# The check of the weights' low halves, two pieces at a time as 32-bit integers

## What is computed

```python
FP4_GRID = jnp.array([0.0, 0.5, 1.0, 1.5, 2.0, 3.0, 4.0, 6.0])
idx = jnp.argmin(jnp.abs(jnp.abs(v)[..., None] - FP4_GRID), axis=-1)
codes = jnp.sign(v) * FP4_GRID[idx]
...
w = codes * jnp.repeat(scales, block_size, axis=0)   # x @ w for q, k, v and the output
```

## Time and profile before

| | |
|---|---|
| runs | 1265.62, 1264.48, 1261.58 us |
| span of the profiled execution | 1275.3 us (no other time of that execution is given) |
| PE busy | 1182.9 us, 93% |
| VectorE, ScalarE, POOL busy | 911.6, 865.0, 664.7 us |
| chain that ended last | PE 64%, DMA 11%, VectorE 10%, issue 7%, ScalarE 6% |
| mean granted TensorE clock | 0.982 |

### The profile page before, as it was taken

How to read it: one execution, slowest core, us unless ns; L and a number is a source line. 1 busy time by engine, 2 the same in 40 slices (tenths; PEclk the granted TensorE clock), 3 DMA queues, 4 the chain that set the end, 5 groups by cost and what they waited for, 6 DMA issues and landing times.

```text
span 1275.3 us, 25192 instructions
## 1 busy us (share of the span) xinstructions
PE 1182.9 (93%) x7600; PEld 836.2 (66%) x7600; DVE 911.6 (71%) x2651; ACT 865.0 (68%) x2316; POOL 664.7 (52%) x746
## 2 busy tenths in 40 slices
PE   3899999999999999999999999999879798989985
PEld 1466666766666676676667666677535477868863
DVE  4887688799789889979988987887757232223336
ACT  3999779878878887887887788788625232323413
POOL 4564334336654655654664565466562523444557
PEclk9999999999999999999999999999989899999998
DMA  7686577867976665565566457456428379898676
GB/s 270 160 213 143 113 131 151 168 151 170 197 174 140 118 123 102 105 123 104 101 108 109 88 97 141 73 100 106 83 58 249 112 207 247 219 234 217 144 197 215
DMA packets 394759, 190.01 MB, mean 149 GB/s; under 512 B 317521, under 2 KB 373303, under 8 KB 394625
## 3 DMA queue, kind: packets, MB, share of 16 engines
q1 hardware_dynamic: 375040, 173.53, 59.7%
q0 software_dynamic: 16416, 11.70, 5.1%
q10 hardware_dynamic: 3168, 3.15, 0.7%
HBM read 75.32 MB, written 64.69 MB: 110 GB/s over the span
## 4 chain that ended last, share of the span: by engine, by line
PE 64%; DMA 11%; DVE 10%; issue 7%; ACT 6%; another core or an unknown queue 1%; SPq 1%; POOL 1%; ACTq 0%; DVEq 0%; POOLq 0%
PE bank L1144 15%; PE bank L1173 14%; PE bank L1188 11%; DMA Y<-W,wix 9%; PE bank L1159 7%; PE bank L1205 7%; PE bank L1237 3%; PE bank L1312 2%; PE bank L1325 2%; PE bank L1355 1%; DVE nm L1581 1%; PE bank L1271 1%; ACT P L1414 1%; DVE PH L1574 1%; DMA X<-in_x 1%
## 5 line engine op out<-in xcount | busy, mean ns | idle before, releaser
L1414 ACT ACTIVATE P<-bank,nm 128x256 f32<-128x256 f32 x512 | 237.9, 471 | 107.3 <-DVE nm L1581 97.1
L1144 PE MATMUL bank<-RB,W 128*128 128x512 f16 x1076 | 275.1, 381 | 5.3 <-DVE W L812 3.9
L1173 PE MATMUL bank<-RB 128*128 128x256 f32 x1024 | 244.6, 382 | 10.2 <-issue 6.9
L1074 POOL TENSOR_SCALAR P<-P,rr 128x256 f32<-128x256 f32 x256 | 121.1, 482 | 252.5 <-DVE rr L1563 244.2
L823 POOL DMA_INDIRECT BUF<-RT,ix x192 | 201.6, 1050 | 72.8 <-issue 37.6
L1173 PEld LDWEIGHTS bank<-RB 128*128 128x128 f32 x1024 | 185.7, 191 | 34.9 <-ACT RB L1385 6.6
L1144 PEld LDWEIGHTS bank<-RB,W 128*128 128x128 f16 x1076 | 105.2, 98 | 123.4 <-issue 8.8
L1581 DVE TENSOR_REDUCE nm<-bank 128x2 f32<-128x512 f32 x256 | 174.2, 681 | 11.0 <-PE bank L1173 8.8
L1205 PE MATMUL bank<-W,O 128*128 128x256 f16 x1060 | 158.8, 275 | 5.2 <-DVE O L1587 5.2
L1095 POOL DMA_INDIRECT Y<-W,wix x64 | 90.9, 1421 | 117.8 <-ACT W L1492 67.5
L1079 POOL TENSOR_TENSOR PH<-P,PH 128x512 f16<-128x512 f32 x86 | 101.2, 1176 | 87.3 <-ACT PH L1430 86.3
(11 more groups left out here) (224 smaller groups left out, 1995.4 us busy)
## 6 DMA issues: line engine op xcount, KB each, us to landing
RB<-in_ewT SPq DMA_DIRECT2D x24, 352.0 KB
BUF<-zrow SPq DMA_DIRECT2D x24, 321.0 KB, 3.3
W<-BUF SPq DMA_DIRECT2D x64, 120.4 KB
HT<-in_ewT SPq DMA_DIRECT2D x18, 352.0 KB
HT<-in_wc SPq DMA_DIRECT2D x24, 256.0 KB, 4.2
HT<-in_ws SPq DMA_DIRECT2D x24, 256.0 KB, 4.7
Y<-zrow SPq DMA_DIRECT2D x20, 256.0 KB
RB<-in_ewd SPq DMA_DIRECT2D x24, 176.0 KB
```

What stands on the lines that cost most here:

```text
L1074: r = eng.tensor_scalar(p, p, rr[:, w % 4, t:t + 1], SP_, ALU.mult, ALU.mult)
L1144: r = eng.matmul(bk_[:, :], W[:, m, a, c * 2048 + h * 128:c * 2048 + (h + 1) * 128], XT[:, bp % 2, b, c, :], start=(k == 0), stop=(k == n ...
L1173: r = eng.matmul(bS[u % 2][:, t * 256:(t + 1) * 256], QK[:, i % 2, 0, q * 256 + t * 128:q * 256 + (t + 1) * 128], QK[:, i % 2, 1, q * 256: ...
L1414: r = eng.activation(P[:, u % 2, t * 256:(t + 1) * 256], bS[u % 2][:, t * 256:(t + 1) * 256], ACT.Exp, bias=nm0[:, u % 4, t:t + 1], accum_ ...
```

## The change

Sixteen checks take the place of 32. Each reads two pieces (the two halves `c` of one chunk `chn`) as 512 integers of 32 bits, where two neighbouring f16 low halves make one integer; the activation is Abs as before, and its output and sum have the size that they had. `CHECK_AT` has 16 entries, one in each of the slots 4 to 17, and two in 19. The flag's maximum runs over 16 columns and waits for 16 checks.

```diff
-CHECK_AT = (0, 1, 1, 2, 2, 2, 3, 3, 4, 5, 5, 5, 8, 8, 8, 9, 9, 10, 12, 12, 12, 14, 15, 15, 15, 16, 16, 17, 18, 19, 19,
- 19)
+CHECK_AT = (4, 5, 6, 7, 8, 9, 10, 11, 12, 13, 14, 15, 16, 17, 19, 19)
...
-        lowsum = C1[:, 0, 0:32]
+        lowsum = C1[:, 0, 0:16]
...
             def check(eng):
+                k = n // 2
                 eng.wait_ge(s["wl"], n + 1)
-                if n:
-                    eng.wait_ge(s["lf"], n)
-                eng.activation(unused[:, :], lo, ACT.Abs, accum_out=lowsum[:, n:n + 1]).then_inc(s["lf"], 1)
+                if k:
+                    eng.wait_ge(s["lf"], k)
+                both = W[:, m, 1, :].bitcast(I32)
+                if m < 3:
+                    both = both.rearrange("p (c n) -> p c n", c=2)[:, :, chn * 256:(chn + 1) * 256]
+                else:
+                    both = both[:, chn * 512:(chn + 1) * 512].rearrange("p (c n) -> p c n", c=2)
+                eng.activation(unused[:, :].rearrange("p (c n) -> p c n", c=2), both, ACT.Abs,
+                               accum_out=lowsum[:, k:k + 1]).then_inc(s["lf"], 1)
...
-            plan["act"].setdefault(CHECK_AT[n], []).append(check)
+            if c == 1:
+                plan["act"].setdefault(CHECK_AT[n // 2], []).append(check)
...
-                eng.wait_ge(s["lf"], 32)
+                eng.wait_ge(s["lf"], 16)
```

## The result

The changed kernel takes **1443.17 us** (median of 4 runs, 1441.09 to 1444.24) against 1263.82 us (4 runs) for the kernel before: 1.143 times as long, 95% interval 1.141 to 1.145, 179 us more. The forecast was 1450.5, in a range of 1440 to 1467.

A forecast was written before the change was run, and what follows sets the result against it. Attention was taken to be bound by PE's number of matmuls, which the flag chooses. On the profiled span: +200 for the longer arm, -6 ahead of the branch, -8 given back, hence 1264.5 + 186 = 1450.5 us, range 1440 to 1467.

The forecast's parts named there:

- What the integer comparison meets: In the new check: low halves of -0 read as nonzero integers, so the flag is 1; chance 0.87.
- The rival that the flag stays 0: At the check: ScalarE keeps a zero's sign, only the first part is left, 1258.5 us; chance 0.09 with that gain.
- The price of the arm: Behind the branch: longer matmul groups, 148 us for Q, K and V plus 52 for the output projection, together 200 us.
- what is given back: Inside the longer arm: PE's waits for other engines shrink, 8 us of 13.4 won back, bounds 0 and 13.4.
- Ahead of the branch: Twelve pairs before the branch: fewer ScalarE checks save PE 6.0 us, between 0 and 10.5.
- the wait ahead of the third scores: PE's 3.11 us wait at 46.11 us, for VectorE's copy of K: some 2.3 us of it go.
- the waits for V behind 100 us: PE's waits at 101.53 (0.87) and 119.36 us (0.65): counted with some small starts of scores as 2.1 us saved.
- nothing is counted for the waits between 54 and 69 us: Ahead of the branch: VectorE is busy 14.80 of 14.80 us there and is late, so no gain was counted.
- nothing reaches PE: Rival: flag stays 0, integers read at 1.13 us, full VectorE takes back the gain; 1263 us, no change; chance 0.04.
- near 43.5 us: Sign ahead of the branch: the third scores start there instead of 46.11 us, with no slow clock behind.
- near 127 us: Sign ahead of the branch: the twelfth pair's end comes there.
- carries over: Whole kernel: the +186 us from the profiled span of 1275.3 us is added to the runs' median of 1264.5 us.

The follow-up runs named there:

- experiments 3 and 4: 3: changed kernel with the low half made as -4 x codes + high, so never -0; 1260.11 us, ratio 0.9988. 4: see experiment 4.
- experiments 1 and 2: 1 is e1, the changed kernel with its flag held at 0; 2 is e2, the kernel before with its flag held at 1.
- e1: Changed kernel with the flag's last step comparing with 1e30, so the flag is 0 whatever the checks find; 1262.04 us, ratio 1.0001.
- experiment 4: Changed kernel with the high half made by VectorE's tensor_scalar instead of ScalarE's activation Copy, prologue order fitted to it; 1277.63 us in one run.
- e2: Kernel before, its own 32 checks kept, with the flag's last step >= 0 instead of > 0, so the flag is 1; 1440.92 us, ratio 1.143.
- e8: Kernel before with its two arms in the other order, so a flag of 0 jumps to the far arm; 1263.55 us, ratio 1.0012.

## Why the prediction was right, and where it was not

**What the integer comparison meets: right, and shown.** -0 in the codes, kept by POOL, turned to +0 in ScalarE's high half, -0 in VectorE's difference, nonzero as an integer: experiments 3 and 4 separate the links, and experiments 1 and 2 show that the flag alone carries the time. The rival that the flag stays 0 is out.

**The price of the arm: right in its counts, 200 us.** In whole pairs it can be checked against e1, whose 111 pairs with two passes are this window:

```profile
138.79:884.40 745.61, 732.24 (x4568) 512.13 (x4567) 650.58 (x1857) 619.93 (x1708) 398.62 (x498) 1.00 0.63 126
```

111 x (8.235 - 6.50) = 192.6 us of matmuls more, and 920.39 - 745.61 = 174.8 measured. The difference is **what is given back: 17.8 us, where the prediction took 8** and held 13.4 for the most there could be. This is the term that was mis-sized most. The three waits of the earlier trace rows (13.4 us) are all gone in the changed kernel: its groups of PE in that window have no idle time at all. The bound was too low because it added up named waits only: 920.39 - 111 x 8.235 leaves 6.3 us for background matmuls, and 745.61 - 111 x 6.50 leaves 24.1, so e1 lost 17.8 us, of which its groups name 12.7. PE's idle time in e1's window is 13.4 us in all; the other 4.4 us stand in no idle time of the profile, and where they lie stays open. The lesson is that a bound is better taken from the window less its floor than from a list of waits.

**Ahead of the branch: wrong, 6 us forecast, none clear of the noise measured.** Only the flag's last step differs between e1 and the changed kernel, and e1's profile shows both sides of the account (PE's timeline, first the kernel before, then e1):

```profile
58.55 1.46 PE L1159 MATMUL bank<-W,RB 128*128 128x512 f16 x6 [0.68 <-DVE RB L1547]
67.41 1.46 PE L1159 MATMUL bank<-W,RB 128*128 128x512 f16 x6 [0.46 <-DVE RB L1547]
```

```profile
44.41 1.97 PE L1180 MATMUL bank<-RB 128*128 128x256 f32 x8 [1.64 <-issue]
52.78 1.97 PE L1180 MATMUL bank<-RB 128*128 128x256 f32 x8 [1.22 <-ACT RB L1392]
57.13 1.46 PE L1166 MATMUL bank<-W,RB 128*128 128x512 f16 x6 [1.09 <-DVE RB L1554]
67.50 1.46 PE L1166 MATMUL bank<-W,RB 128*128 128x512 f16 x6 [1.98 <-DVE RB L1554]
```

Much of the gain came: the wait ahead of the third scores fell from 3.11 to 1.64 us (forecast: 2.3 less), the scores took 1.97 instead of 3.54 us (forecast: 1.6 less), and the waits for V behind 100 us fell by 0.7 us in all (forecast: 2.1 less). Some 3.1 us went again at once: a new wait of 1.22 us for ScalarE's copy of Q, and two waits for V longer by 0.4 and 1.5 us. The failing step is therefore "nothing is counted for the waits between 54 and 69 us": the prediction had said that VectorE is full there and then counted no loss.

In the changed kernel's profile the first gain is smaller still. The first exp of the second pair started at 40.69 instead of 41.67 us, but the third scores 15.3 us behind the first instead of 16.0 (14.2 in e1). VectorE's timeline there (start, us) shows why, with an L602 that took 0.67 us in e1:

```profile
41.83 1.80 DVE L602 SCALAR_TENSOR_TENSOR W<-HT,W 128x512 f16<-128x512 f32 x1
43.55 1.22 DVE L1574 TENSOR_SCALAR r<-rr 128x2 f32<-128x2 f32 x1
...
45.36 0.72 DVE L1549 TENSOR_SCALAR RB<-bank,bqk 128x512 f32<-128x512 f32 x1
```

The full clock behind that wait came here too (1.96 us for the scores), behind an idle time of 2.76 us, though the prediction had tied it to one under 1.5. At 67.92 us V waits 1.99 us for VectorE, and this time the clock falls (V and K take 2.36 and 2.29 us instead of 1.46). What the prediction should have said is that a stretch in which VectorE is full takes back whatever comes to it earlier: its own rival, "nothing reaches PE", was the better account of this part, though with the price of 0.61 us a check and not 1.13. Its signs "near 43.5 us" and "near 127 us" came out at 46.2 and 134.4 us.

**Not foreseen: the jump**, 2.8 us and 11.30 - 8.24 = 3.1 us of slow clock in the profiled execution; some 5 us of it come back at the arm's end (96.2 against 100.8 us).

**The sum.** Against e1, which has the same checks, by spans (1441.7 - 1260.4 = 181.3 us): start and twelve pairs +2.1, jump +3.0, from the arm's first scores to attention's last 954.5 - 771.4 = +183.0, with the slow clock in it, from there to the first expert -4.6, experts and end -2.2. The median was 7.3 us under the forecast: 6 us less gained ahead of the branch and some 6 for jump and clock, against about 10 more given back inside the arm, 5 at its end, and the rest in terms of 1 to 3 us. Two errors of opposite sign made the total look closer than its parts; that it came within 7 us was luck in part.

The profiled execution of the kernel before, on which the sum was made, was 12 us above the median of its runs. Its stretch from the last scores to the first expert took 118.5 us where all other profiles here have 95.9 to 102.5, with a clock of 0.88. That the difference of +186 us "carries over" was therefore safe only because none of its terms came from that stretch.

## What to carry to other kernels

A cheaper test must be equivalent on the data's zeros, not only on its values: reading floats as integers makes -0 count, and 2.7% of the codes here are -0. Ask of any flag that picks a code path what each outcome costs before asking what the test costs; here 10 us of checks stood against an arm of 180. And take the room for a gain from a window less its floor, then name the engine that is full in it: freeing the neighbour of the full engine bought nothing here, while relieving the full one brought the pairs from 102.0 to 95.4 us.

## What the runs showed of the hardware that was not expected

- ScalarE's activation Copy with a scale gives +0 for -0, while VectorE's product keeps the sign (a flag of 1 with the one, of 0 with the other: 1536 and 1076 matmuls of Q and K). This was argued, not known, before experiment 4.
- A jump over an arm of PE's program comes with idle time: 2.80, 2.86 and 2.96 us at the start of the far arm, 2.31 to 2.83 us in eight profiles at the end of the near one, 1.47 in that of the kernel before. The slow clock stood behind the start in some executions: 3.75 us for the scores in the changed kernel and 3.40 in e8, 1.97 in e2. The idle times are alike, so it does not follow from their length alone.
- An activation on 512 32-bit integers takes what one on 512 f16 numbers takes: 634 and 636 ns.
- A VectorE instruction (HT and W in, W out) that started behind one of POOL's tensor operations took 1.75 instead of 0.67 us, and 1.26 instead of 0.17 us with 32 columns; a pair that takes 0.88 us took 2.79.
